# Storing the y rows of two stages from ScalarE's DMA queue instead of SyncE's

## What is computed

```
xn = layernorm(x)
s  = attention(xn)                      # a second layernorm, causal, 512 wide, output projection, residual
gates = softmax(xn @ router_w.T)        # 8 experts, the best 2 kept and renormalised
routed = sum_e gate_e * ((silu(xn @ wg_e) * (xn @ wu_e)) @ wd_e)      # hidden width 352
shared = (silu(xn @ sg) * (xn @ su)) @ sd                             # hidden width 704
out = x + s * silu(routed + shared)
```

## Time and profile before

| what | value |
|---|---|
| median of 3 runs | 1312.19 us (1311.3 to 1313.14) |
| the profiled execution | 1316.26 us, of which the span of the trace is 1314.4 us |
| PE busy | 1236.9 us, 94% of the span |
| VectorE busy | 643.5 us, 49% |
| ScalarE busy | 485.9 us, 37% |
| GpSimd busy | 339.1 us, 26% |
| stores to `shared_rows` / `slot_rows` | 32 / 71, each of 256 KB, 2.3 us from issue to landing |
| DMA queue of SP (q1) / of GpSimd (q0) / of ScalarE (q10) | 133.93 MB / 35.40 MB / 0.02 MB |

### The profile page before, as it was taken

The page is one execution under the profiler, slowest core; times in us unless marked ns, Lnnn a source line. Parts: engine busy times, 40 slices in busy tenths (PEclk is TensorE's granted clock), DMA queues, the critical chain, the costliest instruction groups (busy, mean ns, idle before and its releaser), DMA issues. The chain is left out here.

```text
span 1314.4 us, 23316 instructions
## 1 busy us (share of the span) xinstructions
PE 1236.9 (94%) x7514; PEld 719.6 (55%) x7515; DVE 643.5 (49%) x1285; ACT 485.9 (37%) x909; POOL 339.1 (26%) x430
## 2 busy tenths in 40 slices
PE   7799999999998288999999999998899999999996
PEld 4466666666665155666666666664455455455453
DVE  4755555555545832222323232325765765765454
ACT  4433333333332122333333333333544544544532
POOL 0210000000001521212121212111554554553643
PEclk9899999999999688999999999999999999999999
DMA  8465655555563137444444444444244343333331
GB/s 316 129 138 140 160 155 137 142 142 155 149 151 71 30 91 222 126 116 126 116 128 114 129 113 131 112 114 157 89 160 128 99 159 128 100 93 128 113 104 64
DMA packets 177762, 170.00 MB, mean 129 GB/s; under 512 B 116128, under 2 KB 124328, under 8 KB 177328
## 3 DMA queue, kind: packets, MB, share of 16 engines
q1 hardware_dynamic: 166880, 133.93, 35.9%
q0 software_dynamic: 10800, 35.40, 9.4%
q10 hardware_dynamic: 32, 0.02, 0.0%
HBM read 96.88 MB, written 45.88 MB: 109 GB/s over the span
## 5 line engine op out<-in xcount | busy, mean ns | idle before, releaser
L409 PE MATMUL pair<-arena 128*128 (+1 forms) x3240 | 510.8, 315 | 0.2 <-issue 0.2
L409 PEld LDWEIGHTS pair<-arena 128*128 128x128 f16 x3240 | 319.2, 99 | 165.8 <-issue 1.3
L416 PE MATMUL bank<-arena 128*128 (+1 forms) x1215 | 288.0, 383 | 12.9 <-ACT arena L857 7.8
L416 PEld LDWEIGHTS bank<-arena 128*128 128x128 f16 x1215 | 117.1, 98 | 138.5 <-issue 18.5
L1509 PE MATMUL pair<-arena 128*128 128x512 f16 x672 | 154.0, 385 | 2.9 <-PEq L1104 2.9
L1260 DVE SCALAR_TENSOR_TENSOR arena<-pair,arena 128x352 f32<-128x352 f32 x71 | 37.2, 524 | 192.7 <-ACT arena L1224 192.7
L837 ACT ACTIVATE arena<-pair 128x352 f32<-128x352 f32 x64 | 29.7, 464 | 217.4 <-PE pair L409 217.4
L1509 PEld LDWEIGHTS pair<-arena 128*128 128x128 f16 x672 | 66.5, 99 | 77.9 <-issue 7.4
L192 POOL TENSOR_TENSOR root_seed<-var_eps,minus_half 128x1 f32<-128x1 f32 x32 | 17.6, 550 | 348.5 <-DVE var_eps L201 348.4
L1552 PE MATMUL bank<-arena 128*128 128x512 f16 x432 | 98.5, 379 | 5.1 <-DVE arena L1687 5.1
L1524 PE MATMUL pair<-arena 128*128 128x512 f16 (+3 forms) x576 | 98.8, 326 | 0.0
(11 more groups left out here) (170 smaller groups left out, 1334.5 us busy)
## 6 DMA issues: line engine op xcount, KB each, us to landing
slot_rows<-arena SPq DMA_DIRECT2D x71, 256.0 KB, 2.3
arena<-in_L_attn_x_dram SPq DMA_DIRECT2D x64, 256.0 KB, 3.0
xn_rows<-arena SPq DMA_DIRECT2D x32, 256.0 KB, 3.2
shared_rows<-arena SPq DMA_DIRECT2D x32, 256.0 KB, 2.3
arena<-in_L_attn_x_dram SPq DMA_DIRECT2D x8, 1024.0 KB, 8.4
arena<-shared_rows SPq DMA_DIRECT2D x32, 256.0 KB, 3.1
out_dram<-arena SPq DMA_DIRECT2D x32, 256.0 KB, 2.0
arena<-in_L_ffn_wg_dram SPq DMA_DIRECT2D x32, 176.0 KB, 3.3
```

The costliest lines, as they stand in the source:

```text
L409: last = pe.matmul(bank[:, 0:H], xt[:, a, c, :], weights(c, b, col), start=(c == 0 and i == 0), stop=(c == KC - 1 and i == 2))
L416: last = pe.matmul(bank[:, :], ht[:, a, c, :], weights(c, b), start=(start and c == 0 and i == 0), stop=(stop and c == HC - 1 and i == 2))
```

## The change

The two `store_y` functions of SP are taken out, with all their calls. In each `y_copy` of ScalarE two instructions are added behind the copy: a wait until the copy has signalled `y_ready`, and the DMA that stores the rows. The DMA has the same source, target, size and semaphore as before. ScalarE issues 32 of these stores in the shared stage and 71 in the routed stage.

```diff
@@ stages1and2, SP
-                    def store_y(t):
-                        sp.wait_ge(y_ready, t + 1)
-                        sp.dma_start(shared_rows[bass.ds(t * P, P), :], y_out).then_inc(y_stored, 16)
...
-                        if not early(t, 2):
-                            store_y(t - 2)
...
-                    store_y(NT - 2)
-                    store_y(NT - 1)
@@ stages1and2, ScalarE
                         nc.scalar.activation(y_out, y_bank[:, :], ACT.Copy, scale=Y_SCALE).then_inc(y_ready, 1)
+                        act.wait_ge(y_ready, t + 1)
+                        act.dma_start(shared_rows[bass.ds(t * P, P), :], y_out).then_inc(y_stored, 16)
@@ stage3, SP
-                    def store_y(j, u):
-                        sp.wait_ge(y_ready, j + 1)
-                        sp.dma_start(slot_rows[bass.ds(j * P, P), :], bufs["y", u]).then_inc(y_stored[u], 16)
-
                     def slot_tile(j, u):
-                        if not early(j, 3):
-                            store_y(j - 3, 1 - u)
...
-                    for j in range(T - 3, T):
-                        store_y(j, j % 2)
@@ stage3, ScalarE
                         nc.scalar.activation(bufs["y", u], y_bank[u][:, :], ACT.Copy, scale=Y_SCALE).then_inc(y_ready, 1)
+                        act.wait_ge(y_ready, j + 1)
+                        act.dma_start(slot_rows[bass.ds(j * P, P), :], bufs["y", u]).then_inc(y_stored[u], 16)
```

## The result

The changed kernel takes 1318.26 us (median of 20 runs, 1314.58 to 1322.30), the kernel before 1313.70 us in the 20 runs beside them (1309.91 to 1318.43). The ratio is 1.0033 [1.0022, 1.0043]: slower by 0.33%, some 4.3 us. The forecast was no change that can be measured, 1313.1 us, with a range up to 1316.5. The loss is clear of the noise and the median lies above the range. Of the distance to the forecast, 1.5 us is the kernel before itself, which has 1313.70 us in these runs and had 1312.19 in the three that the forecast started from. The change alone is +4.3 us against the +0.9 forecast, and against the sum's upper bound of +3.0.

What follows compares the result with a forecast made beforehand. PE's own work was taken to set the pace in 600 us of the span, untouched by the change. The terms 0.63 + 0.3 + 0 gave +0.9 us on the median 1312.19, so 1313.1 us, range 1310.3 to 1316.5.

Steps and rivals of the forecast that it cites:

- the sum's upper bound: Whole kernel: the most that the terms together were taken to cost, +3.0 us, against +0.9 expected.
- the burst: Stage-4 loads, 490 to 508 us: store y(2) passes transpose turn(4), +0.63 us, bounds -0.63 and 2.06.
- Steady tiles: Shared and routed stages: the store holds ScalarE about 1.35 us after each copy, hidden by cover; cost nothing.
- the first rival: Shared stage: ScalarE held over 1.76 us, router waits for `x_low`, 11 us lost, 1323 us; chance 0.07.
- the second rival: Stores on the second queue slow every transpose; some +3 us, 1315.2, if the burst meets its bound; chance 0.06.
- cover of 2.17 us for `h_high`: Routed stage: transpose lands 2.17 us before `h_high` needs it; a store takes 0.63 us, so cost nothing.
- The transpose near 417 us: Shared stage, transpose issued at 417.80: y(29)'s store now goes out beside it, +0.3 us, bounds -1.3 and +0.63.
- The barrier at 905 us: End of routed stage: last store frees ScalarE at 904.80, before VectorE ends at 905.00; cost 0, at most +0.3 us.
- Relief: Transpose at 417.80 gives back 1.3 us, y(1) leaving SP's queue 0.63: 1310.3; chance 0.10, over 2.6 us gain 0.04.

Runs made afterwards that it cites:

- E5: Kernel before, with only the routed stage's store y(1) issued by ScalarE: 1312.11 us, ratio 0.9993.
- E6: Kernel before, with only the routed stage's store y(2) issued by ScalarE: 1317.64 us, ratio 1.0036.
- E10: E6's kernel, with GpSimd holding the gather of slot 9 until turn(4) has landed: 1314.84 us, ratio 1.0009.
- E11: Changed kernel, with GpSimd holding the gather of slot 9 until turn(4) has landed: 1315.42 us, ratio 1.0013.
- E12: Kernel before, with GpSimd holding the gather of slot 9 until turn(4) has landed: 1313.93 us, ratio 1.0000.
- E8: Changed kernel, with the three stage-4 loads cut into 16 of 256 KB, one behind each of turn(4) to turn(19): 1308.45 us, ratio 0.9965.
- E2: Kernel before, with only the 71 stores of the routed stage issued by ScalarE: 1317.23 us, ratio 1.0032.
- E3: Changed kernel, but the routed stage's stores y(0), y(1) and y(2) stay on SP's queue: 1314.47 us, ratio 1.0010.
- E1: Kernel before, with only the 32 stores of the shared stage issued by ScalarE: 1314.45 us, ratio 1.0010.
- E7: Kernel before, with the three stage-4 loads cut into 16 of 256 KB, one behind each of turn(4) to turn(19): 1308.45 us, ratio 0.9964.
- E9: Kernel before, with the three stage-4 loads issued by ScalarE behind its `h_high` of slot 3: 1321.09 us, ratio 1.0055.

## Why the prediction was wrong

**The step that failed** is the burst: "I take y(2)'s whole transfer as new ahead of turn(4): +0.63 us", with an upper bound of 2.06. That y(2) passes turn(4) was right. The size of the term was not, and a second term was missing. y(2) alone makes the loss (E5, E6), and it does pass turn(4). But PE's wait grew by 3.8 us. y(2) in front makes turn(4) start 1.7 us later instead of 0.63. The rest, 2.0 us against before, comes from a transfer that stood nowhere in the sum: the gather of slot 9, now beside turn(4). With the gather held 3.0 us are gone, and 0.6 to 1.5 us of y(2)'s part are left (E10, E11). The gather is slowed too. In the kernel before it took 7.7 us from its issue to its landing, and in the changed kernel 9.8:

```profile
arena<-xn_rows,arena POOLq DMA_INDIRECT x1, 7.7
```

```profile
arena<-xn_rows,arena POOLq DMA_INDIRECT x1, 9.8
```

**The bounds.** The range of this term came from rates of the burst (419 and 127 GB/s). The row that was nearest to what happened was turn(4)'s own: 13.6 us for a transfer that usually takes 2.8. I read it as "stands behind the loads", and the packets bear that out: 9.5 of the 13.6 us went by before its first one moved. But the transfer itself then took 3.6 us where E12, with no gather beside it, took 2.4. The row thus held a price for company, and the bounds had none.

**Steady tiles: cost nothing, as predicted.** In the changed kernel's tile of the shared stage (timeline; L849 is `y_copy`, L824 `x_high`, L766 the router):

```profile
304.68 0.60 ACT L849 ACTIVATE arena<-bank 128x512 f32<-128x512 f32 x1 [0.33 <-PE bank L416]
305.44 0.34 ACTq L851 DMA_DIRECT2D shared_rows<-arena  x1
305.97 0.59 ACT L824 CAST arena<-bank 128x512 f16<-128x512 f32 x1 [0.69 <-ACT arena L849]
...
308.35 0.50 PEld L766 LDWEIGHTS bank<-rw_split,arena 128*128 128x128 f16 x12
```

The issue begins 0.16 us after the copy ends (305.44 - 305.28) and takes 0.34 us. I had taken 0.75 and 0.60. `x_high` starts 1.29 us behind the copy's start where it was 0.52, so it is 0.77 us late and not 1.43. The weight load comes 3.67 us behind the copy's start as before (308.35 - 304.68; 309.96 - 306.29). All 32 and 71 issues are alike (instructions of one line; the count stands behind the x, the durations are in ns):

```profile
L851 ACTq DMA_DIRECT2D shared_rows<-arena x32: 338/357/396, 69.9 to 437.1; - x32
```

```profile
L1203 ACTq DMA_DIRECT2D slot_rows<-arena x71: 338/362/380, 481.1 to 905.0; - x71
```

Gap and issue together, 0.16 + 0.40 = 0.56 us at the most, stay far from the 1.76 us at which the first rival decides, so that rival is out.

**Every transpose slowed: half true, and free.** This was the second rival. In the shared stage it holds. Of the DMAs issued from 130 to 400 us, the changed kernel's transposes landed after 3.8 us, those before after 2.8:

```profile
arena<-arena SPq DMA_TRANSPOSE x45, 3.8
```

```profile
arena<-arena SPq DMA_TRANSPOSE x46, 2.8
```

In the routed stage it is another matter. In the changed kernel ScalarE waits for the transpose in 67 of 71 slots (chain of waits: who waits, for what, us, times, longest), where before it did in 3. A slot of it, from the silu (L1212) to `h_high` (L1196):

```profile
ACT arena L1196 <- DMA arena<-arena: 199.3, 67, 13.2
```

```profile
601.08 0.47 ACT L1212 ACTIVATE arena<-pair 128x352 f32<-128x352 f32 x1 [0.76 <-PE pair L409]
...
604.95 0.48 ACT L1196 CAST arena<-arena 128x352 f16<-128x352 f32 x1 [3.40 <-DMA arena<-arena]
...
606.84 2.10 PE L416 MATMUL bank<-arena 128*128 x9
```

E8 has all the same stores on ScalarE's queue and no burst. There the same two rows (L1220, L1204), and the landing of the transposes issued from 530 to 860 us, read:

```profile
598.41 0.46 ACT L1220 ACTIVATE arena<-pair 128x352 f32<-128x352 f32 x1 [2.57 <-PE pair L409]
599.54 0.48 ACT L1204 CAST arena<-arena 128x352 f16<-128x352 f32 x1 [0.67 <-DVE arena L1256]
```

```profile
arena<-arena SPq DMA_TRANSPOSE x56, 2.8
```

`h_high` starts 1.13 us behind its silu in E8, as in the kernel before, and 3.87 us behind it in the changed kernel. There the transpose was issued at 599.9 and landed 5.0 us later, at 604.95. Each `h_high` waits for the transpose ahead of it, its own transpose is issued late for that reason, and it now goes out together with the store and the gather, which makes it slow again. That account is read from the timeline; no run moved the store or the gather of a steady slot. What E8 shows is that the same stores without the burst don't have the pattern. With the burst it lasts for the rest of the stage. I looked for it in every kernel: it is there in the four that have both the burst and the later stores of the routed stage on ScalarE's queue (the changed kernel, E2, E3, E11), and in none of the others, where `h_high` is back at 1.13 us within five slots of the burst. It costs no time that can be measured, since PE reaches the matmul that needs the data at 606.84, 1.9 us after the landing. E3 has the pattern and a ratio of 1.0010; E11 has it and E10 has not, 1.0013 against 1.0009. But the prediction's cover of 2.17 us for `h_high` was wholly used up, and no step of mine had seen that a delay could keep itself alive.

**The transpose near 417 us.** Its landing came 4.6 us after its issue instead of 4.1, where +0.3 us had been taken. But it was issued at 415.65, which is 2.15 us earlier than before, while the executions are 1.62 us apart in all of this stage. The `h_high` that it frees starts 1.62 us ahead of before's 421.92, so in this execution the place cost nothing:

```profile
420.30 0.48 ACT L835 CAST arena<-arena 128x352 f16<-128x352 f32 x1 [3.81 <-DMA arena<-arena]
```

E1, which holds this term, measures 1.0010 [0.9997, 1.0022].

**The barrier at 905 us.** The changed timeline there:

```profile
905.02 0.34 ACTq L1203 DMA_DIRECT2D slot_rows<-arena  x1
...
905.38 0.69 DVE L1025 TENSOR_TENSOR arena<-arena 128x512 f16<-128x512 f32 x1
```

ScalarE is through at 905.36, and VectorE works until 906.07, so the last store holds nobody up, as predicted. VectorE's end is 1.07 us behind before's 905.00, though, and the slots up to 880 us were 0.72 us behind: 0.35 us were lost near this end. E2, E3 and E11, with the same stores, lose under 0.05 us there, and the changed kernel has it made good by 930 us.

**Relief** came only as E5's shorter wait, in one execution. Its time is within 0.2% of before, and y(2) buries it in the whole change.

**What isn't accounted for.** The stretch of the burst explains 3.2 of the 4.3 us in the two profiled executions; the rest is within the interval (1.0022 is 2.9 us). The nine matmuls behind the wait take 3.10 to 4.02 us where PE waited 3.47 us or more, and 2.10 to 2.12 in E5, E7 and E8, since the granted clock is down to 0.50 after a long wait (508 to 512 us, in both kernels). Before and after are nearly alike in this, 4.02 and 3.79 us; it is a part of what E7 gains. Each wait here is from one execution, and a single one of the kernel before isn't a sure measure of it. From the first to the second of the two multiplications shown above E5 gains 3.7 us and E7 6.7 on the profiled execution of before, but their medians are only 0.8 and 4.5 us below before's.

## What to carry to other kernels

Before a store or load goes to another queue, list what is in flight beside each DMA transpose on which an engine waits, and not only what is ahead of it in its own queue; a steady stage can hide a microsecond of it in every tile, while one burst passes it on to TensorE. After the burst, look whether the steady pattern is still the one of before. Cut a bulk load that has time into pieces between such transfers: here this was worth 0.36%, and it made the question of the queue disappear.

## What the hardware showed that was not expected

- A DMA transpose of 128 x 6 x 128 float16 landed in 2.8 us in the median of the shared stage with the stores in its own queue, in 3.8 us with them on another queue, in 13.6 us once behind 4 MB of loads in its own queue, and in 20.9 us once with the loads on another queue beside it (E9).
- One burst left the routed stage in another steady pattern for some 60 slots: transposes that landed in about 5 us instead of 2.8, with the stores on the same queue in both (changed kernel against E8).
- Such a transpose and a 256 KB gather slow each other, by more than their packets' turns: 3.1 us of PE's wait went away with the gather held (E10), the gather took 9.8 us instead of 7.7, and 12 of its 64 packets took 2.1 to 3.9 us where 0.16 is usual.
- ScalarE's issue of a 256 KB store takes 0.34 to 0.36 us and begins 0.16 us behind its copy. SP's issue of the same store took 0.57 us in the median.
- SP's issue of turn(4) took 4.29 us in the changed kernel and 1.22 us in E6, with the same wait of PE behind it.
